# New orders for four engines: a Mamba mixer and a quantised feed-forward layer on one core

## What is computed

```python
x = x + mixer(ctx_1024, layernorm(x))     # B=4, L=256, 256 channels, 16 states
    xc  = silu(conv4(in_proj(ctx)) + conv_b)
    dt  = softplus(dt_proj(low rank part of x_proj(xc)) + dt_b)
    state[t] = state[t-1] * exp(dt[t] * A) + dt[t] * xc[t] * B[t]   # 16 states per channel
    y   = (sum over states of state[t] * C[t] + D * xc) * silu(z)
x = x + ffn(layernorm(x))                 # 256 -> 1024 -> 256
    h = layer_norm(gelu(silu(bitlinear(x, w1, b1)))) * g + b
    out = bitlinear(h, w2, b2)            # rows quantised to 8 bits, weights to -1, 0, 1
```

## Time and profile before

| | us |
|---|---|
| median of 3 runs | 200.37 (200.09 to 201.26) |
| the profiled execution | 200.04 |
| its span in the profile | 198.1 |
| VectorE busy | 167.5 (85%) |
| ScalarE busy | 161.1 (81%), of it 29 table loads 37.2 |
| TensorE busy | 159.7 (81%) |
| GpSimd busy | 127.8 (65%), of it 32 products 77.5 |

### The profile page before, as it was taken

How to read it: one execution, slowest core, us unless ns; L and a number is a source line. 1 busy time by engine, 2 the same in 40 slices (tenths; PEclk the granted TensorE clock), 3 DMA queues, 4 the chain that set the end, 5 groups by cost and what they waited for, 6 DMA issues and landing times.

```text
span 198.1 us, 3315 instructions
## 1 busy us (share of the span) xinstructions
PE 159.7 (81%) x1161; PEld 118.8 (60%) x1167; DVE 167.5 (85%) x225; ACT 161.1 (81%) x255; POOL 127.8 (65%) x117
## 2 busy tenths in 40 slices
PE   5987999989979699969695796938997948791693
PEld 3756968678768577746494574707873625341472
DVE  0569829479999999999999999999997889999741
ACT  2178989999979998559999799929899986899421
POOL 4002575559576757729879498946989985447860
PEclk9997999999999959999999999995899995797569
...
GB/s 136 341 4 332 388 418 271 4 73 322 229 28 129 86 60 55 206 109 23 195 0 85 132 100 115 0 28 0 0 3 0 26 0 0 0 30 26 3 39 67
DMA packets 20192, 20.12 MB, mean 102 GB/s; under 512 B 13448, under 2 KB 16976, under 8 KB 19536
## 3 DMA queue, kind: packets, MB, share of 16 engines
...
q10 hardware_dynamic: 592, 0.77, 1.4%
...
## 4 chain that ended last, share of the span: by engine, by line
DVE 33%; PE 29%; issue 16%; POOL 10%; ACT 8%; DMA 2%; DVEq 0%; POOLq 0%; ACTq 0%
DVE st L956 13%; PE ps L517 9%; PE ps L555 5%; PE ps L454 4%; POOL st L829 4%; DVE stats L1026 4%; ACT dA L681 3%; DVE xc L991 3%; DVE am L1051 3%; PE ps L483 3%; PE ps L432 2%; DMA inw_sb<-inwT 2%; POOL w_raw L891 2%; DVE w_raw L963 2%; PE ps L465 2%
## 5 line engine op out<-in xcount | busy, mean ns | idle before, releaser
L829 POOL TENSOR_TENSOR st<-st,bc 128x1024 f32<-128x1024 f32 x32 | 77.5, 2437 | 27.8 <-DVE st L956 27.6
L956 DVE TENSOR_TENSOR_SCAN st<-dA,ps 128x1024 f32<-128x1024 f32 x32 | 71.7, 2271 | 8.6 <-PE ps L517 7.3
L681 ACT ACTIVATE dA<-dt,negA 128x255 f32<-128x255 f32 x128 | 52.7, 494 | 0.6 <-POOL negA L810 0.6
L517 PE MATMUL ps<-diagB,dtuT 64*128 64x128 f32 x512 | 44.5, 307 | 10.6 <-DVE st L956 9.8
L517 PEld LDWEIGHTS ps<-diagB,dtuT 64*128 64x128 f32 x512 | 35.1, 202 | 22.8 <-DVE st L956 12.5
L778 ACT ACT_TABLE_LOAD x29 | 37.2, 1283 | 0.5
L555 PE MATMUL ps<-id_f,st 128*128 128x128 f32 x256 | 34.9, 288 | 2.7 <-POOL st L829 2.7
L555 PEld LDWEIGHTS ps<-id_f,st 128*128 128x128 f32 x256 | 30.5, 149 | 5.9 <-POOL st L829 3.9
L592 PE MATMUL ps<-rows_sb,diag 128*128 128x512 f32 x32 | 17.2, 664 | 1.8 <-ACT q2T L750 1.2
L616 PE MATMUL ps<-id_f,w_raw 128*128 128x128 f32 x64 | 10.7, 322 | 9.1 <-POOL w_raw L891 6.8
L616 PEld LDWEIGHTS ps<-id_f,w_raw 128*128 128x128 f32 x64 | 8.6, 165 | 11.3 <-issue 11.0
...
## 6 DMA issues: line engine op xcount, KB each, us to landing
...
```

Source lines behind the costliest of these rows:

```text
L517: mm = nc.tensor.matmul(o[:, i:i + SG // 2, t, r, :], dtuT[rows, b % 2, h, t, :], diagB[rows, b % 2, t, n, :], start=True, stop=True)
L681: e = nc.scalar.activation(dA[:, k % DA_RING, i * L + 1:(i + 1) * L], dt[:, h, b, 1:L], ACT.Exp, scale=negA[:, h, n:n + 1])
L829: tt(s, s, bc[:, ng].rearrange("p s l -> p (s l)"), ALU.mult).then_inc(prod_done, 1)
L956: nc.vector.tensor_tensor_scan(st[:, k % ST_RING, :], dA[:, k % DA_RING, :], slot(k), 0.0, ALU.mult, ALU.add).then_inc(scanned, 1)
```

## The change

Only the strings of the four tables are others. Each table holds the same words as before, in another order or at another step k; functions, buffers, semaphores and transfers are as they were. On VectorE, `times_u:2`, `ln1:0`, `quant1:0` and both `clip_weights` now stand at step 10 with the first gates, `bn2:0` at 14, `gain:0` at 17. On TensorE, `scale_rest:1` stands behind `convolve:3` to `5`. On ScalarE the second sequence's preparation comes at step 4, the third's and fourth's at step 11.

```diff
--- before
+++ after
@@ -54,74 +54,74 @@
 VECTOR_AT = (
     "spread_b:1 z_norm:1 times_half:1 spread_b:2 spread_b:3",
     "",
-    "",
     "times_u:1",
     "",
+    "",
+    "",
+    "",
+    "",
     "wmean:0",
     "",
-    "",
-    "clip_weights:0",
-    "",
-    "",
-    "gate:0 gate:1 x1:0 x1:1 times_u:2 ln1:0",
-    "",
-    "quant1:0",
-    "",
-    "",
-    "times_u:3 clip_weights:1",
-    "",
-    "gate:2 x1:2 bn2:0 gate:3",
-    "",
-    "x1:3 ln1:1 gain:0",
-    "bn2:1",
+    "times_u:2 gate:0 gate:1 x1:0 x1:1 ln1:0 quant1:0 clip_weights:0 clip_weights:1",
+    "",
+    "",
+    "",
+    "times_u:3 bn2:0",
+    "",
+    "",
+    "gain:0",
+    "gate:2 gate:3 x1:2 x1:3 amax2:0",
+    "bn2:1 ln1:1",
     "quant1:1",
-    "",
-    "amax2:0 scales2:0 gain:1",
-    "",
-    "gate:4 x1:4 gate:5 x1:5 ln1:2 res:0 bn2:2",
-    "amax2:1 scales2:1 gain:2",
-    "",
-    "amax2:2",
-    "scales2:2 bn2:3 quant1:2",
+    "scales2:0",
+    "gain:1",
+    "",
+    "",
+    "bn2:2 amax2:1",
+    "",
+    "gain:2 res:0 scales2:1 gate:4 gate:5 x1:4 x1:5",
+    "ln1:2 amax2:2 scales2:2",
+    "bn2:3 quant1:2",
     "gain:3",
-    "res:1 amax2:3 bn2:4 gate:6 gate:7 x1:6 x1:7 scales2:3 ln1:3 quant1:3 gain:4 bn2:5 amax2:4 gain:5 res:2 "
-    "scales2:4 amax2:5 bn2:6 res:3 gain:6 scales2:5 amax2:6 bn2:7 scales2:6 gain:7 res:4 amax2:7 scales2:7 "
-    "res:5 res:6 res:7",
+    "",
+    "amax2:3 bn2:4 gate:6 gate:7 x1:6 x1:7 scales2:3 res:1 ln1:3 res:2 quant1:3 bn2:5 gain:4 gain:5 amax2:4 "
+    "bn2:6 scales2:4 amax2:5 gain:6 scales2:5 bn2:7 amax2:6 res:3 scales2:6 gain:7 res:4 amax2:7 res:5 "
+    "scales2:7 res:6 res:7",
 )
 SCALAR_AT = (
     "",
     "",
     "",
     "",
-    "",
     "silu_u:1 silu_z:0 silu_u:2 copy_xd:1 delta:1 sum_weights:0 copy_half:1",
-    "sum_weights:1 copy_xd:2",
+    "",
+    "copy_xd:2",
     "",
     "copy_du:1",
-    "scale_weights:0",
-    "",
-    "",
-    "delta:2 silu_u:3 copy_z:0",
-    "copy_xd:3",
-    "",
-    "copy_du:2",
-    "",
-    "",
-    "",
-    "delta:3 scale_weights:1 silu_z:1 copy_q1:0 silu_z:2 silu_z:3 copy_z:1 silu:0 gelu:0",
-    "",
-    "copy_du:3",
-    "norm:0 silu:1 gelu:1 copy_z:2",
-    "",
-    "copy_z:3 square:0 norm:1 copy_q1:1",
-    "",
-    "silu:2 scale2:0 gelu:2 copy_q2:0",
-    "",
-    "square:1",
-    "norm:2",
-    "scale2:1 silu:3 square:2 gelu:3",
-    "copy_q2:1 scale2:2 norm:3 copy_q2:2 copy_q1:2",
-    "silu:4 gelu:4 square:3 silu:5 scale2:3 copy_q2:3 gelu:5 copy_q1:3 square:4 silu:6 gelu:6 square:5 silu:7 "
+    "sum_weights:1",
+    "",
+    "delta:2 scale_weights:0 copy_z:0 silu_u:3 silu_z:1 copy_xd:3 scale_weights:1 copy_du:2 delta:3",
+    "copy_q1:0",
+    "",
+    "",
+    "silu:0 gelu:0 copy_z:1",
+    "",
+    "",
+    "copy_du:3 norm:0",
+    "silu_z:2 silu_z:3 silu:1 gelu:1",
+    "copy_z:2",
+    "square:0 copy_z:3",
+    "",
+    "",
+    "norm:1 copy_q1:1",
+    "scale2:0 silu:2 gelu:2",
+    "copy_q2:0",
+    "square:1 norm:2",
+    "",
+    "scale2:1 square:2 silu:3 gelu:3 copy_q2:1 scale2:2",
+    "copy_q2:2 norm:3",
+    "copy_q1:2",
+    "silu:4 gelu:4 square:3 silu:5 gelu:5 scale2:3 copy_q2:3 copy_q1:3 silu:6 square:4 gelu:6 square:5 silu:7 "
     "gelu:7 square:6 copy_q2:4 copy_q2:5 square:7 copy_q2:6 copy_q2:7",
 )
 POOL_AT = (
@@ -135,68 +135,68 @@
     "",
     "",
     "",
-    "",
-    "root1:0 add_b2:0",
-    "",
-    "",
-    "",
-    "",
-    "",
-    "",
-    "root2a:0",
-    "",
-    "root1:1 shift:0",
-    "root2a:1",
-    "root2b:0",
-    "",
-    "out_scale:0 add_b2:1",
+    "root1:0",
+    "",
+    "",
+    "",
+    "add_b2:0 root2a:0",
+    "",
+    "shift:0",
+    "",
+    "",
+    "root1:1 add_b2:1 root2a:1 root2b:0",
+    "",
+    "out_scale:0",
+    "",
     "shift:1",
-    "root1:2 root2a:2 root2b:1",
-    "shift:2 out_scale:1",
-    "root2b:2",
+    "root2a:2",
+    "root2b:1 shift:2",
+    "root2b:2 root1:2",
+    "",
     "root2a:3",
-    "",
-    "shift:3",
-    "out_scale:2 root2b:3 out_scale:3 add_b2:2 root1:3 root2a:4 add_b2:3 root2a:5 root2b:4 out_scale:4 "
-    "scale_last:4 root2a:6 root2b:5 scale_last:5 root2b:6 root2a:7 scale_last:6 out_scale:5 root2b:7 "
+    "out_scale:1 shift:3",
+    "",
+    "",
+    "root2b:3 out_scale:2 add_b2:2 root1:3 out_scale:3 root2a:4 add_b2:3 root2a:5 root2b:4 out_scale:4 "
+    "root2b:5 root2a:6 scale_last:4 scale_last:5 root2b:6 root2a:7 scale_last:6 out_scale:5 root2b:7 "
     "scale_last:7 out_scale:6 out_scale:7",
 )
 PE_AT = (
-    "turn_half:0 convolve:2 scale_b:0 scale_b:1 scale_rest:0 scale_rest:1 convolve:3 convolve:4 scale_b:2 "
-    "convolve:5 xdbl:1 scale_rest:2 dtraw:1 scale_b:3 scale_rest:3 turn_half:1",
-    "convolve:6 scale_b:4 scale_b:5 scale_rest:4 scale_rest:5 xdbl:2",
-    "wsum:0",
-    "scale_b:6 turn_du:1 scale_rest:6",
+    "turn_half:0 convolve:2 scale_b:0 scale_b:1 scale_rest:0 convolve:3 convolve:4 convolve:5 xdbl:1 scale_b:2 "
+    "scale_rest:1 dtraw:1",
+    "turn_half:1 scale_rest:2 scale_b:3 convolve:6 scale_rest:3 scale_b:4 xdbl:2 scale_rest:4",
+    "scale_b:5 scale_rest:5 turn_du:1",
+    "scale_b:6 scale_rest:6",
     "scale_b:7 scale_rest:7",
-    "dtraw:2 scale_b:8 scale_b:9 scale_rest:8 scale_rest:9",
-    "",
-    "convolve:7 scale_b:10 scale_rest:10 turn_z:0",
-    "scale_b:11 scale_rest:11 scale_b:12 xdbl:3",
-    "",
-    "",
-    "turn_du:2 scale_rest:12 scale_b:13 dtraw:3 scale_rest:13 scale_b:14",
-    "scale_rest:14",
-    "scale_b:15 scale_rest:15 scale_b:16 scale_rest:16 turn_q1:0",
-    "",
-    "bias:0 turn_z:1 scale_b:17 mm1:0 scale_rest:17 scale_b:18 turn_du:3",
-    "scale_rest:18 scale_b:19 bias:1 scale_rest:19 mm1:1 turn_z:2 scale_b:20",
-    "scale_rest:20 scale_b:21",
-    "",
-    "scale_rest:21",
-    "turn_z:3",
-    "scale_b:22 scale_b:23 scale_rest:22 scale_rest:23 turn_q1:1 bias:2",
-    "scale_b:24 mm1:2 scale_rest:24 scale_b:25 scale_rest:25",
-    "",
-    "turn_q2:0 scale_b:26 scale_rest:26 scale_b:27 scale_rest:27 mm2:0",
-    "bias:3 mm1:3 scale_b:28 scale_rest:28",
-    "",
-    "scale_b:29 scale_rest:29 turn_q2:1 scale_b:30 scale_rest:30",
-    "scale_b:31 scale_rest:31",
-    "turn_q1:2 turn_q2:2 bias:4 mm1:4 mm2:1",
-    "",
-    "bias:5",
-    "mm1:5 turn_q2:3 turn_q1:3 bias:6 mm1:6 mm2:2 bias:7 mm2:3 mm1:7 turn_q2:4 turn_q2:5 mm2:4 turn_q2:6 mm2:5 "
-    "turn_q2:7 mm2:6 mm2:7",
+    "scale_b:8 wsum:0 scale_rest:8 scale_b:9 dtraw:2",
+    "scale_rest:9",
+    "turn_z:0",
+    "convolve:7 xdbl:3 scale_b:10 turn_du:2",
+    "scale_b:11 dtraw:3 scale_rest:10",
+    "turn_q1:0 scale_rest:11 bias:0 turn_z:1 mm1:0 scale_b:12 scale_rest:12 scale_b:13 scale_rest:13",
+    "scale_b:14",
+    "scale_rest:14 scale_b:15",
+    "bias:1 scale_rest:15 turn_du:3 mm1:1 scale_b:16 scale_rest:16",
+    "scale_b:17 scale_rest:17",
+    "scale_b:18",
+    "scale_rest:18 scale_b:19 turn_z:2 scale_rest:19",
+    "",
+    "scale_b:20 scale_rest:20 turn_z:3",
+    "scale_b:21 turn_q1:1 bias:2 scale_rest:21 scale_b:22 scale_rest:22",
+    "",
+    "scale_b:23 mm1:2 scale_rest:23 scale_b:24 scale_rest:24",
+    "scale_b:25 scale_rest:25 turn_q2:0 scale_b:26 scale_rest:26",
+    "",
+    "mm2:0 bias:3 scale_b:27 scale_rest:27 scale_b:28 scale_rest:28 mm1:3",
+    "scale_b:29 turn_q2:1",
+    "",
+    "scale_rest:29 scale_b:30 scale_rest:30 turn_q2:2 turn_q1:2",
+    "bias:4 scale_b:31 scale_rest:31",
+    "mm1:4 mm2:1",
+    "bias:5 mm1:5",
+    "",
+    "mm2:2 turn_q2:3 turn_q1:3 bias:6 mm1:6 mm2:3 bias:7 mm1:7 turn_q2:4 turn_q2:5 mm2:4 turn_q2:6 mm2:5 mm2:6 "
+    "turn_q2:7 mm2:7",
 )
```

More of the change, by code:

```diff
@@ L56 @@
     "",
+    "times_u:1",
     "",
-    "times_u:1",
+    "",
+    "",
+    "",
     "",
@@ L61 @@
     "",
-    "",
-    "clip_weights:0",
+    "times_u:2 gate:0 gate:1 x1:0 x1:1 ln1:0 quant1:0 clip_weights:0 clip_weights:1",
     "",
     "",
-    "gate:0 gate:1 x1:0 x1:1 times_u:2 ln1:0",
     "",
-    "quant1:0",
+    "times_u:3 bn2:0",
     "",
     "",
-    "times_u:3 clip_weights:1",
+    "gain:0",
+    "gate:2 gate:3 x1:2 x1:3 amax2:0",
+    "bn2:1 ln1:1",
+    "quant1:1",
+    "scales2:0",
+    "gain:1",
     "",
-    "gate:2 x1:2 bn2:0 gate:3",
     "",
-    "x1:3 ln1:1 gain:0",
-    "bn2:1",
-    "quant1:1",
-    "",
-    "amax2:0 scales2:0 gain:1",
-    "",
-    "gate:4 x1:4 gate:5 x1:5 ln1:2 res:0 bn2:2",
-    "amax2:1 scales2:1 gain:2",
-    "",
-    "amax2:2",
-    "scales2:2 bn2:3 quant1:2",
-    "gain:3",
-    "res:1 amax2:3 bn2:4 gate:6 gate:7 x1:6 x1:7 scales2:3 ln1:3 quant1:3 gain:4 bn2:5 amax2:4 gain:5 res:2 "
-    "scales2:4 amax2:5 bn2:6 res:3 gain:6 scales2:5 amax2:6 bn2:7 scales2:6 gain:7 res:4 amax2:7 scales2:7 "
-    "res:5 res:6 res:7",
+    "bn2:2 amax2:1",
+    "",
+    "gain:2 res:0 scales2:1 gate:4 gate:5 x1:4 x1:5",
+    "ln1:2 amax2:2 scales2:2",
+    "bn2:3 quant1:2",
+    "gain:3",
+    "",
+    "amax2:3 bn2:4 gate:6 gate:7 x1:6 x1:7 scales2:3 res:1 ln1:3 res:2 quant1:3 bn2:5 gain:4 gain:5 amax2:4 "
```

(77 more changed lines are left out.)

## The result

The changed kernel takes 188.6 us (median of 4 runs, 188.09 to 189.16), the kernel before beside it 200.2: a ratio of 0.941 [0.937, 0.945]. That is 11.6 us less, where 5.4 were forecast. The direction was right, the size was not, and what follows finds the terms of the sum that were off.

The account below looks back on a forecast made before the run. VectorE was taken as the bound, losing time to collisions with GpSimd's products: -15.6 + 3.0 + 3.6 + 2.4 + 1.2 = -5.4 us on 200.04, 194.6; with the runs' median 0.33 higher, 195.0 us, range 190.0 to 201.0.

Parts of the forecast that it names:

- The collisions: Up to the last scan, VectorE operations waiting for GpSimd products in progress: 15.6 us lost, counted as -15.6.
- step 1: Block after scan 9: times_u:2, gates, x1, ln1:0, quant1:0 and both clips run clear of products; 5.0, 1.99 and 1.43 us go.
- Step 2: Later places: quant1:1, quant1:2, gain:1 and a backlog of products at ln1 still collide, +3.0 us (bounds 0 and 8.2).
- Step 3: First scans: with scale_rest:1 later, scan 1 waits 5.4 us; waiting up to scan 9 totals 8.9 us.
- Steps 4 and 5: New later waits bring VectorE's idle time to 13.9 us against 10.3 (+3.6); handoffs between engines add 2.4 us.
- step 5: Handoffs: some 20 changes of engine on the path, at 0.12 us each, add 2.4 us (1.0 to 5.2).
- the walk: New orders worked through with profiled durations, next engine starting at once; it gave 13.9 us of VectorE idle time.
- Step 6: After the last scan: shift:3 delays GpSimd's last products, ending 4.7 us behind that scan instead of 3.5, +1.2 us.
- What was given no cost: Stretch behind the last gates: a few neighbours exchanged, VectorE's long operations there colliding with no product; costed at nothing.
- The rivals: Three alternative outcomes: residual collisions of one-input operations (chance 0.12), ScalarE taking over (0.14), a larger gain (0.10).
- ScalarE doesn't take over: Rival, chance 0.14: late ScalarE work delays bn2 and gains ahead of scans, 11.7 us in all, giving up to 204.7 us.
- The larger gain: Rival, chance 0.10: no residual collisions and new waits inside today's 10.3 us, -12.0 us, 188.4 us; stopping around 190 expected.

## Why the prediction was wrong in size

*The collisions and step 1: right in the mechanism, and nearly in size.* 15.6 us were summed, and 15.7 went when the products were taken out. The parts agree less well than the sums: the clean clip is 1.22 us, not 1.05 (0.3 too much), and two prolonged rows were left out, L1089 with 0.78 us and L1004 with 0.37, which take 0.15 and 0.14 beside products of 8 columns (0.9 together). Of step 1 only times_u:2 came otherwise: product 8 was still running when it began, and it took 0.97 for 0.67.

*Step 2: the size by luck.* 3.0 was taken and 3.0 measured, but at quant1:1, quant1:2 and gain:1, the places named, nothing collided, and a backlog of products at ln1 cost a pair of L991 only 0.2. The rest lies elsewhere: times_u:2 and times_u:3, behind scans 9 and 13, each began while the product before (8 and 12) was running (0.97 and 1.23 for 0.67), gain:0, held to be clean, took 1.67 for 1.22, and L1089, which the prediction didn't look at, lost 1.9.

*Step 3: the waits of the first scans came near what was worked out.* Scan 1 waited 5.14 for 5.4, and all waits up to scan 9 came to 7.4 for 8.9. That scan 10 then started at 64.91 for "near 65" is in part luck: the 1.5 us of waiting that didn't come were made up by what L1089 and times_u:2 lost (2.2).

*Steps 4 and 5, and their place beside step 2: these failed.* The miss lies behind scan 10: the last scan was to end at 148 to 151 and ended at 143.40. The waits and handoffs that were to come on top of the old idle time were put at 3.6 + 2.4 = 6.0 us; measured, VectorE's idle time grew by 0.3. Against 13.9 + 2.4 = 16.3 us of idle time foreseen stand 10.6: 1.5 less ahead of scans 1 to 9, 2.7 less at the later places (2.3 for 1.0 + 1.3 + 1.3 + 1.4 = 5.0; bn2:0 waited 0.58 for 1.3, scan 12 not at all), and 0.9 of pauses too short to be listed where 2.4 were added for handoffs. Such pauses come to 0.9 in the kernel before as well, so step 5 added what today's idle time held already. With 0.3 in place of 6.0 the prediction's own sum is -15.6 + 3.0 + 0.3 + 1.2 = -11.1, 188.9 us for the profiled execution, which took 188.1.

The run of the new order with products of 8 columns shows how the waits could be so much shorter than the walk had them. There the residue of 3.0 is gone, VectorE idles for 13.6 us, near the walk's 13.9 (bn2:0 waits 1.49 for 1.3), and the stretch from first to last scan is as long, 122.3 us in both. As far as this run can stand for the changed kernel, for its products are short as well, residue and waits are not two costs: what is held up reaches the next wait later and finds it shorter. The sum counted 3.0 + 3.6 + 2.4 = 9.0 for what measured 3.3; of the 5.7 too much, 3.0 are the residue counted beside the waits that it hides, and the rest is handoffs (1.5) and waits (some 1.2) that were too large by themselves.

The walk also laid durations end to end. The Trainium skill ("Perfetto Trace Analysis", section "Optimizing Scalar/DVE Operations") says that the part of a profiled latency in which the write is acknowledged overlaps with the next instruction; the trace agrees, with 0.08 us at each of the three joints of the scans at 64.91. What this did to the walk's waits no run here shows.

*Step 6: right.* Its result of 4.7 us behind the last scan was measured to the tenth, though its own figures, 9.5 less 4.6, give 4.9.

*What was given no cost* gained 0.9 in the last stretch, and why stays open. A collision of L1020 there is gone (1.10 us for 0.29), but two of L1040 now wait behind GpSimd's scaling (L891) and take 1.95 for 1.28, so VectorE's long operations do collide there, if not with a product. TensorE's clock, for which as many falls were assumed as before, had none in mid-kernel; in the kernel before, the waits of VectorE behind scan 9 that end with TensorE come to only 0.4 us, so the two falls there had cost VectorE little.

*The rivals.* Before the last scan no one-input operation collides any more but L1089 and, by 0.2 us, L991: the order keeps them apart too, whatever it says of two-input ones. ScalarE doesn't take over: ahead of the last scan bn2 and the gains wait 0.6 us in all where 11.7 were the price, and the scans wait 0.2 for their exponentials. The prediction's reason for stopping near 190 was sound in kind: ScalarE did run out of pauses, at 188.6. The larger gain comes out near the time by luck: its conditions were no residue and waits within 10.3, and there were 3.0 of residue and 10.6 of waits; it also held 2.4 of handoffs that didn't come.

What the experiments add is where the gain can't be split. The block without the other tables costs 8.5 us, most of it in waits for TensorE, and gains nothing; moving only the clips costs 9. VectorE's whole new table with the three old ones, and the reverse, weren't run: by their tables two engines would wait for each other for ever. In the first, clip_weights:1 stands ahead of scan 10 and needs scale_weights:1, which ScalarE has behind the exponentials of unit 18, and these need a buffer that scan 12 frees; in the second, TensorE has turn_q1:0 ahead of scale_rest:11, and VectorE has quant1:0, which it needs, behind scan 12. So how much each engine's order is worth alone isn't known.
